# Attention scores dealt one by one over two rings of three PSUM banks, sums copied and casts placed elsewhere in ScalarE's order

## The reference

```
q = einsum('oc,bct->bot', Wq, target) + bq        # target: x after the first norm, as (16, 256, 512)
k = einsum('oc,bcs->bos', Wk, source) + bk        # source: ctx_2048, (16, 256, 512)
v = einsum('oc,bcs->bos', Wv, source) + bv
# 16 heads of 16 channels, 512 target and 512 source positions
dot  = einsum('bhdt,bhds->bhts', q, k) / sqrt(16)
dot  = mask * dot - (1 - mask) * 1e6
amap = softmax(dot, axis=-1) * mask
out  = einsum('bhts,bhds->bhdt', amap, v)
```

## Time and profile before

| | |
|---|---|
| median of 3 runs | 3223.22 us (3222.08 to 3226.16) |
| profiled execution, its own time | 3223.97 us |
| its span | 3222.1 us |
| TensorE matmul busy | 3000.6 us (93%) |
| VectorE busy | 2795.2 us (87%) |
| ScalarE busy | 2410.8 us (75%) |
| GpSimd busy | 2094.2 us (65%) |
| first scores, first to last start | 1763.2 to 2743.3 us |
| second scores, first to last start | 1815.4 to 2790.9 us |
| mean granted TensorE clock | 0.979 of full speed |

### The profile page before, as it was taken

One profiled execution on the slowest core, in us unless ns is written; L12 is line 12 of the kernel. 1 busy time (PEld: TensorE's weight loads), 2 busy tenths in 40 slices (PEclk: granted clock), 3 DMA queues, 4 the chain that ended last, 5 costly groups with the idle time before them and its releaser, 6 DMA issues. The chain is left out here.

```text
span 3222.1 us, 47346 instructions
## 1 busy us (share of the span) xinstructions
PE 3000.6 (93%) x16101; PEld 1827.8 (57%) x16134; DVE 2795.2 (87%) x3637; ACT 2410.8 (75%) x4531; POOL 2094.2 (65%) x1207
## 2 busy tenths in 40 slices
PE   7899999999999999999985899999999999699998
PEld 5777677777777677777753344444444443244444
DVE  6999999999999999999996878777887877288886
ACT  4888888888888888888872377677677667577786
POOL 5999999999999999999995243343344333100000
PEclk9999999999999999999996899999999999899999
DMA  4102220222012210222024455555556553221111
GB/s 173 45 32 79 80 73 18 79 83 79 26 65 79 80 62 29 79 80 83 15 96 137 148 171 168 186 158 177 177 154 179 168 178 92 82 93 47 46 42 36
DMA packets 164385, 311.93 MB, mean 97 GB/s; under 512 B 22736, under 2 KB 80208, under 8 KB 164000
## 3 DMA queue, kind: packets, MB, share of 16 engines
q1 hardware_dynamic: 158784, 299.53, 29.0%
q10 hardware_dynamic: 5360, 9.38, 1.0%
HBM read 217.16 MB, written 91.69 MB: 96 GB/s over the span
## 5 line engine op out<-in xcount | busy, mean ns | idle before, releaser
L830 POOL TENSOR_TENSOR bu<-du,bc 128x1024 f32<-128x1024 f32 x512 | 1198.9, 2370 | 30.4 <-DMA bc<-bc_scratch 28.5
L708 ACT ACTIVATE states<-dt,negA 128x256 f32<-128x256 f32 x2048 | 853.1, 463 | 238.7 <-DVE hc L926 227.9
L914 DVE TENSOR_TENSOR_SCAN states<-states,bu 128x512 f32<-128x512 f32 x704 | 821.5, 1213 | 10.6 <-ACT states L708 8.7
L1565 DVE TENSOR_REDUCE mmax<-s_ps 128x2 f32<-128x1024 f32 x512 | 624.8, 1224 | 205.6 <-PE s_ps L1284 186.7
L1409 ACT ACTIVATE pt<-s_ps 128x512 f32<-128x512 f32 x1024 | 573.5, 598 | 293.6 <-PE s_ps L1293 280.4
L926 DVE TENSOR_TENSOR hc<-states,bc 128x512 f32<-128x512 f32 x704 | 446.4, 676 | 0.4 <-DMA bc<-bc_scratch 0.4
L526 PEld LDWEIGHTS y_ps<-id_sb,hc 128*128 128x128 f32 x2816 | 331.5, 143 | 121.7 <-DVE hc L926 56.1
L526 PE MATMUL y_ps<-id_sb,hc 128*128 128x128 f32 x2816 | 377.5, 277 | 22.1 <-DVE hc L926 22.1
L1293 PE MATMUL s_ps<-qst,kst 105*128 105x512 bf16 x1024 | 379.1, 384 | 15.5 <-ACT pt L1409 5.1
L839 POOL TENSOR_TENSOR hp<-hp,bc 128x1024 f32<-128x1024 f32 x160 | 379.5, 2372 | 1.8 <-DVE hp L914 1.8
L914 DVE TENSOR_TENSOR_SCAN hp<-states,bu 128x512 f32<-128x512 f32 x320 | 372.5, 1206 | 5.2 <-ACT states L708 5.2
(11 more groups left out here) (172 smaller groups left out, 4237.4 us busy)
## 6 DMA issues: line engine op xcount, KB each, us to landing
bc<-bc_scratch SPq DMA_DIRECT2D x128, 512.0 KB, 5.1
stack_d<-parts SPq DMA_DIRECT2D x180, 256.0 KB, 3.0
qst<-stack_d SPq DMA_DIRECT2D x64, 384.0 KB
kst<-stack_d SPq DMA_DIRECT2D x64, 384.0 KB
x<-xres SPq DMA_DIRECT2D x31, 512.0 KB, 5.3
w_raw<-in_w_ffn SPq DMA_DIRECT2D x48, 256.0 KB, 2.7
w_raw<-in_w_ffn SPq DMA_DIRECT2D x16, 768.0 KB, 7.3
xT_sb<-in_xT SPq DMA_DIRECT2D x16, 512.0 KB, 6.0
```

Source lines behind the costliest of these rows:

```text
L708: a = act.activation(states[:, bank, first:first + SEQ], dt[:, t, :], ACT.Exp, scale=negA[:, t, c * NS + n:c * NS + n + 1])
L830: pool.tensor_tensor(bu[:, buf, :].rearrange("p (n l) -> p n l", n=NS), du[:, t % (2 * GRP):t % (2 * GRP) + 1, :].to_broadcast([P, NS, SEQ ...
L914: dve.tensor_tensor_scan(dst, src, bu[:, BU_OF[k][0], cols], 0.0, ALU.mult, ALU.add).then_inc(scan_done, 1)
L1565: dve.tensor_reduce(mmax[:, u // HG, c:c + 2], s1_ps[:, pair], AX.X, ALU.max).then_inc(s1_free, 1)
```

## The change

`s1_ps` and `s2_ps` become rings of three banks each. First scores are dealt, signalled, reduced and freed one tile at a time. On ScalarE the exponentials of half 0 come first in every head; the casts of k and q follow them; the copy of the sums moves to heads 3, 7, 11 and 15, after half 0; the casts of the turned maxima move behind half 1 of the head in which the maxima are transposed (0, 9, 14).

```
+S_BANKS = 3
...
-        s1_ps = ps("s1_ps", [P, 2, 2, HID])
-        s2_ps = ps("s2_ps", [P, 2, HID])
+        s1_ps = ps("s1_ps", [P, S_BANKS, HID])
+        s2_ps = ps("s2_ps", [P, S_BANKS, HID])
...
+        def score(batch, u, tt):
+            return (batch * HEADS + u) * TT + tt
...
-            def scores_max(s, par, u, pair):
-                if pair == 0 and u % HG == 0:
+            def scores_max(s, par, u, tt):
+                if tt == 0 and u % HG == 0:
                     pe.wait_ge(stack_in[u // HG], (s + 1) * (4 * 16))
-                if not (isinstance(s, int) and s == 0 and u == 0):
-                    pe.wait_ge(s1_free, s * 32 + u * 2 + pair - 1)
-                for i in range(2):
-                    tt = pair * 2 + i
-                    m = pe.matmul(s1_ps[:, pair, i, :], qst[0:ROWS1, par, u, tt * P:(tt + 1) * P],
-                                  kst[0:ROWS1, par, u, :], start=True, stop=True)
-                m.then_inc(s1_ready, 1)
+                n = score(s, u, tt)
+                if n >= S_BANKS:
+                    pe.wait_ge(s1_free, n - S_BANKS + 1)
+                pe.matmul(s1_ps[:, n % S_BANKS, :], qst[0:ROWS1, par, u, tt * P:(tt + 1) * P],
+                          kst[0:ROWS1, par, u, :], start=True, stop=True).then_inc(s1_ready, 1)
...
-                if not (isinstance(b, int) and b == 0 and u == 0 and st < 2):
-                    pe.wait_ge(exp_done, b * 64 + u * TT + st - 1)
-                pe.matmul(s2_ps[:, st % 2, :], kst[0:ROWS2, par, u, st * P:(st + 1) * P],
+                n = score(b, u, st)
+                if n >= S_BANKS:
+                    pe.wait_ge(exp_done, n - S_BANKS + 1)
+                pe.matmul(s2_ps[:, n % S_BANKS, :], kst[0:ROWS2, par, u, st * P:(st + 1) * P],
                           qst[0:ROWS2, par, u, :], start=True, stop=True).then_inc(s2_ready, 1)
...
-                        if tt % 2 == 0 and active(s):
-                            scores_max(s, 1 - par, u, tt // 2)
+                        if active(s):
+                            scores_max(s, 1 - par, u, tt)
...
                 for u in range(HEADS):
+                    if active(b):
+                        exponentials(b, u, 0)
                     for kind, unit in SPLIT_AT.items():
                         if u - unit in (0, 1) and active(f):
                             round_part(kind, f, u - unit)
-
-                    if u % HG == 0:
-                        g, batch = (u // HG - 2, b) if u >= 2 * HG else (u // HG + 2, n)
+                    if u % HG == HG - 1:
+                        g, batch = (u // HG - 1, b) if u >= HG else (HGROUPS - 1, n)
                         if active(batch):
                             copy_values(batch, g)
                     if active(b):
-                        exponentials(b, u, 0)
+                        exponentials(b, u, 1)
                     for unit, kind, idx, off in MISC:
-                        if unit == u - 1 and kind == "m" and active(b + off):
+                        if unit == u and kind == "m" and active(b + off):
...
-                    if active(b):
-                        exponentials(b, u, 1)
...
-            def row_max(s, u, pair):
-                dve.wait_ge(s1_ready, s * 32 + u * 2 + pair + 1)
-                c = u % HG * TT + 2 * pair
-                dve.tensor_reduce(mmax[:, u // HG, c:c + 2], s1_ps[:, pair], AX.X, ALU.max).then_inc(s1_free, 1)
+            def row_max(s, u, tt):
+                n, c = score(s, u, tt), u % HG * TT + tt
+                dve.wait_ge(s1_ready, n + 1)
+                dve.tensor_reduce(mmax[:, u // HG, c:c + 1], s1_ps[:, n % S_BANKS], AX.X, ALU.max).then_inc(s1_free, 1)
...
-                    if active(s):
-                        row_max(s, u, 1)
+                    for tt in range(1, TT):
+                        if active(s):
+                            row_max(s, u, tt)
```

More of the change, by code:

```diff
@@ L1358, in shared @@
                 elif part == 0:
-                    pe.wait_ge(s1_free, batch * 32 + (MAXIMA[idx][-1] + 1) * HG * 2)
+                    pe.wait_ge(s1_free, score(batch, (MAXIMA[idx][-1] + 1) * HG, 0))
                     for i, g in enumerate(MAXIMA[idx]):
@@ L1408, in exponentials @@
                     act.wait_ge(s2_ready, b * 64 + u * TT + st + 1)
-                    act.activation(pt[:, g % 2, u % HG, st, :], s2_ps[:, st % 2], ACT.Exp).then_inc(exp_done, 1)
+                    act.activation(pt[:, g % 2, u % HG, st, :], s2_ps[:, score(b, u, st) % S_BANKS], ACT.Exp).then_inc(exp_done, 1)
             def load_ctx(f, par):
```

## The result

The changed kernel takes 3176.7 us (median of 4 runs, 3173.55 to 3176.83) against 3223.47 for the kernel before on the same chip: ratio 0.9851, 95% interval 0.9837 to 0.9866, so 1.5% faster. The forecast was 3181, with a range of 3171 to 3205.

A forecast was written before the change was run, and what follows sets the result against it. TensorE with its waits was taken as the bound, 3.2 us per body to win. 14 bodies at −2.4 (−33.6), body without projections −2.5, first +1.8 and last −8 made −42.3: 3181 us, range 3171 to 3205.

The forecast's parts named there:

- Copy: Two value blocks per body wait for ScalarE's copy of the sums; moving it wins all 1.3 us.
- Second scores' third bank: Second scores wait for exponentials; a ring of three banks instead of two wins all 1.9 us per body.
- the 0.2 for VectorE's lag: Small new waits per body where VectorE lags: 0.2 us lost.
- First scores: VectorE's 64 smaller reductions take 0.69 each, adding 2.4 us per body; head 1's fourth score waits 0.5 behind the statistics.
- rival B: Late context load or key stores replace the waits, costing 1.0 to 1.9 us per body: 3195 to 3208; chance 0.14.
- 0.2 left: Slack between the key casts' stores landing and the query cast on ScalarE: 0.2 us left, costing nothing.
- still over 2 us left: Slack of the maxima's rows before second scores need them at the change of bodies: over 2 us.
- 0.1 for the context load: Context load, issued later in head 14 and used sooner, keeps 0.2 to 0.3 us spare; 0.1 per body charged.
- Last body: Second scores alone: three banks cut the last body from 46 us to 38, −8; half would be −4.
- C: Reductions' fixed cost doesn't halve as taken, or VectorE's lag reaches more first scores: 3190 to 3200; chance 0.09.
- D: No change: the rings' gain is given back in VectorE's queue, last body's 8 us halved: 3217 to 3229; chance 0.06.
- E: Slower: VectorE becomes the bound if a small reduction costs over 0.86 us instead of 0.69; chance 0.05.

The follow-up runs named there:

- e1: The kernel before with only ScalarE's order taken from the change, all banks as they were: 60.77 us per body, 3202.6 us.
- e2: The changed kernel with ScalarE's order of before, so both rings of three banks alone: 61.23 us per body, 3200.6 us.
- e3: The changed kernel with two banks for second scores and ScalarE's order of before, first scores still in three: 61.65 us per body, 3213.2 us.
- second profile: The changed kernel, unaltered, run and profiled again on the same chip: 59.53 us per regular body, 3176.45 us.
- e4: The changed kernel with the norm statistics split over the ends of heads 0 and 1: 59.27 us per body, 3169.8 us.
- e9: The changed kernel with the copy of the sums back at the start of heads 0, 4, 8 and 12: 60.18 us per body, 3186.8 us.

## Why the prediction was right, and where not

**The bound and the size to be won.** The prediction counted 3.2 us of losses per body from starts, with TensorE and its waits as the bound. It is so: the period fell by 2.82 and 0.48 are left, which adds up to 3.3. But its two terms, 1.3 and 1.9, divide it wrongly: the same trace shows 1.59 at value blocks and 1.58 at second scores.

**Copy.** Forecast 1.3, measured 1.58 with the banks of before and 1.70 with the rings. The term was undersized because I read it from two rows of the waits, not from starts. Timeline of TensorE before, head 8, ahead of the earlier trace rows:

```profile
2096.96 0.39 PE L1293 MATMUL s_ps<-qst,kst 105*128 105x512 bf16 x1
```

The value block starts at 2098.47, 1.51 later where 0.31 is usual: 1.2 us, and 0.27 at the change of bodies and 0.11 in head 4 make 1.6, which e1 wins whole. With the rings the wait at the change of bodies grows (0.27 to 0.52, e2), as TensorE arrives earlier.

**Second scores' third bank: the step that failed.** "I take all 1.9 as won", and by the bank. Taken together the rings give 1.12 (e2) to 1.24 (change against e1), where I had 1.9 − 0.5 − 0.2 = 1.2, so the sum came out right, in part by luck: the 1.9 was 1.58 at second scores and 0.16 at key products, and the 0.2 for VectorE's lag did not come. What failed is the cause. Dealing single first scores gives 0.70 net with two banks (e3), which I had booked as cost alone; 0.71 of second scores' waits go by it. The third bank takes the other 0.87. Its net is 0.42 (e2 against e3), as the waits for the copy and behind the statistics grow meanwhile from 1.69 to 2.18. I had not asked what stands between two second scores on TensorE once first scores are dealt. What a third bank would give without dealing was not run.

**First scores.** 0.69 us per small reduction was taken and 0.686 is the mean; 0.60 from start to start against 0.61. VectorE's work grew by 2.3 us in a body, forecast 2.4. The place and size of the one new wait, head 1's fourth score at 0.5 us, are as forecast: 0.48. The Trainium skill's rule of about 125 ns per operation on PSUM ("Perfetto Trace Analysis", Optimizing Scalar/DVE Operations) would have made 0.66, an estimate. Measured, 512 elements more take 0.54 (1.14 less 0.60), which leaves 0.06 of the 0.60, so the trace disagrees with it for this instruction. The same section of the Trainium skill says that smaller instructions may let work finish sooner where the engine isn't saturated but holds others up. No run shows that by itself: e3 made the reductions smaller and dealt the scores in one edit, and what it won stands mainly in waits for ScalarE (0.71), not for VectorE (0.16, the key products of head 2).

**Casts and transfers.** The distance from the last key cast (2080.01) to the first query cast (2089.88) is 9.87, forecast 9.8, and in a regular body no cast waits for the stores. But in four bodies it does, by 0.26 to 1.66, which is one of the prediction's own signs of being wrong, and rival B's mechanism: the two exponentials behind the cast are late, and TensorE loses 1.8 us in body 0, 0.4 in body 6 and 0.1 in body 13. "0.2 left" was too little. Of the two transfers named as tight or safe, I had them the wrong way round in the first profile: the context load held nothing, and the maxima's rows, with "still over 2 us left", held the first second score of four bodies (0, as before the change, 1, 6 and 9). Their stores now take longer. Landing times of those stores, before and after, min, median, max:

```profile
DMA to landing us min/median/max: 1.4/3.7/7.8
```

```profile
DMA to landing us min/median/max: 1.4/5.9/8.3
```

I had taken one body's times for all. In the trace before, the loads of the maxima's rows already start anywhere from 55.7 to 57.5 us into a body; after, from 55.3 to 57.6, in a body 2.8 us shorter. In the second profile and in e4 the context load does hold TensorE. All irregular bodies together cost 2.7 us (834.88 less 58.28 and 13 × 59.53), 0.3 of it the longer statistics of body 8; that is 0.2 per body, where I had 0.1 for the context load and nothing for the other two.

**Ends.** Last body −6.9 for −8, first +1.2 for +1.8, the latter at a different granted clock (0.76 and 0.66), so it isn't a clean measure of that term. The body without projections gave 4.5 where I took the steady body's 2.5: every head is light there, so TensorE meets every wait, and I had not looked at it by itself. By the table the order alone gives 0.8 of it (e1), dealing 1.7 (e3), both rings 3.3 (e2). In all −42.3 forecast and −47.1 seen, of which −48.3 lie inside the attention phase.

**Rivals.** B (a transfer takes over) is real but small: 1.8 us in body 0, and 0.1 to 1.0 in four others. C, D and E are out: a small reduction costs 0.69, and VectorE is busy 51.9 of 59.5. How much of e4's shorter first body is the statistics' and how much the clock's stays open.

## What to carry to other kernels

When two streams of short instructions share an engine that takes them in the program's order, alternate them one by one and count banks as well: of second scores' waits, dealing took 0.71 us per body with no bank more, a third bank 0.87 (net of new waits elsewhere 0.70 and 0.42), and the bank paid most where one stream stood alone (5 to 7 us in one body). A copy that frees a buffer belongs where its input is just complete, not behind other work of its engine; that was the largest net part (1.6 to 1.7 us per body), though with rings of three, moving the casts from ahead of it won 1.05 of that by itself (e2 against e9). After a gain of some 5% in a loop, take every transfer's slack again from the starts and move the issues, for what was 2 to 3 us of slack is then chance.

## What had not been expected of the hardware

Six banks split 4 and 2, 3 and 3, or 2 and 4 give 59.95, 59.53 and 61.65 us per body. The same transfers in the same order differ from body to body by over a us in when they land (the load of the maxima's rows starts 55.3 to 57.6 us into a body), while the compute engines repeat to 0.02 us: the irregular bodies were numbers 5, 6, 8 and 13 in one profile and 3, 6, 8 and 10 in another.
